# Window and global attention on one core: biases, output copies and shift pieces move to other engines, the ring of exponentials grows from eight to twelve units

## What is computed

```python
# layer 0, per window of 49 tokens
qn, kn = q / |q|, k / |k|
attn = softmax(qn @ kn.T * exp(min(logit_scale, log 100)) + bias[rel_index]);  h = proj(attn @ v)
h = relu(group_norm(x + h));  z = relu(group_norm(h + w2 @ relu(w1 @ group_norm(h) + b1) + b2))
# layer 1, per image, n = 3136 tokens, d = 16
q, k, v = split(w_qkv @ z)
attn = softmax(einsum("bhdn,bhdm->bhnm", q, k) * d ** -0.5)
out = w_proj @ einsum("bhnm,bhdm->bhdn", attn, v) + z
```

## Time and profile before

| | us |
|---|---|
| median of 3 runs | 8928.1 (8922.54 to 8929.63) |
| profiled execution, its run | 8930.84 |
| profiled execution, its span | 8928.7 |
| busy: PE, PEld | 8444.4, 4093.4 |
| busy: DVE, ACT, POOL | 7493.6, 6326.0, 835.1 |
| mean granted clock of TensorE | 0.98 |

### The profile page before, as it was taken

The page is one execution under the profiler, slowest core; times in us unless marked ns, Lnnn a source line. Parts: engine busy times, 40 slices in busy tenths (PEclk is TensorE's granted clock), DMA queues, the critical chain, the costliest instruction groups (busy, mean ns, idle before and its releaser), DMA issues.

```text
span 8928.7 us, 373040 instructions
## 1 busy us (share of the span) xinstructions
PE 8444.4 (95%) x145926; PEld 4093.4 (46%) x145926; DVE 7493.6 (84%) x9622; ACT 6326.0 (71%) x13874; POOL 835.1 (9%) x676
## 2 busy tenths in 40 slices
PE   4799999999999999999999999999999999999997
PEld 2344444444444444444444444444444444444443
DVE  3788888888888888888888888888888888888885
ACT  1377677776767777677776777767777776777776
POOL 3110101001010010101101010010100101010000
PEclk8799999999999999999999999999999999999998
DMA  1201102020110201102011110201102011020110
GB/s 32 40 14 27 27 20 37 12 38 18 28 28 15 41 15 27 27 13 42 14 26 27 23 34 12 42 17 25 28 15 40 15 27 27 13 43 13 29 23 19
DMA packets 123209, 226.00 MB, mean 25 GB/s; under 512 B 57218, under 2 KB 89090, under 8 KB 121354
## 3 DMA queue, kind: packets, MB, share of 16 engines
q1 hardware_dynamic: 121490, 201.52, 12.4%
HBM read 67.50 MB, written 42.73 MB: 12 GB/s over the span
## 4 chain that ended last, share of the span: by engine, by line
PE 76%; DVE 12%; issue 5%; SPq 3%; DMA 3%; ACT 1%; DVEq 0%; POOL 0%; POOLq 0%; ACTq 0%
PE PS L1251 22%; PE PS L1110 21%; PE PS L1263 20%; DVE small L891 7%; PE PS L1151 3%; PE PS L1171 3%; DVE small L930 2%; PE PS L1203 1%; DMA tok_unit<-in_query_ident 1%; PE PS L1141 1%; PE PS L1212 1%; SPq L619 1%; PE PS L1160 1%; PE PS L1182 1%; DVE win_scores L933 1%
## 5 line engine op out<-in xcount | busy, mean ns | idle before, releaser
L829 ACT ACTIVATE exps<-PS 128x392 f32<-128x392 f32 x12800 | 5502.0, 500 | 2087.5 <-PE PS L1251 1659.7
L891 DVE TENSOR_REDUCE small<-PS 128x1 f32<-128x784 f32 x6400 | 5878.1, 966 | 698.8 <-PE PS L1110 662.2
L1110 PE MATMUL PS<-k_stack,q_stack 96*32 96x392 bf16 x51200 | 3250.9, 334 | 225.5 <-DVE small L891 85.1
L1251 PE MATMUL PS<-q_stack,k_stack 99*32 99x392 bf16 x51200 | 3397.4, 333 | 26.9 <-ACT exps L829 12.6
L1263 PE MATMUL PS<-exps,v_all 128*32 128x392 f32 x25600 | 2687.4, 495 | 1.2 <-issue 1.0
L1251 PEld LDWEIGHTS PS<-q_stack,k_stack 99*32 99x32 bf16 x51200 | 1349.1, 95 | 1782.3 <-ACT exps L829 1033.2
L1110 PEld LDWEIGHTS PS<-k_stack,q_stack 96*32 96x32 bf16 x51200 | 1193.6, 96 | 1774.9 <-DVE small L891 967.6
L1263 PEld LDWEIGHTS PS<-exps,v_all 128*32 128x32 f32 x25600 | 749.6, 110 | 333.4 <-ACT exps L829 48.5
L729 POOL TENSOR_TENSOR win_scores<-win_scores,small 128x784 f32<-128x784 f32 x256 | 384.2, 1502 | 1860.0 <-DVE small L942 1860.0
L930 DVE TENSOR_REDUCE small<-PS 128x16 f32<-128x784 f32 x256 | 247.5, 967 | 182.6 <-PE PS L1151 181.2
L1151 PE MATMUL PS<-kmask,tok_unit 113*64 113x392 f32 (+1 forms) x2048 | 375.4, 502 | 16.5 <-DMA tok_unit<-in_query_ident 15.7
(11 more groups left out here) (113 smaller groups left out, 3044.9 us busy)
## 6 DMA issues: line engine op xcount, KB each, us to landing
q_stack<-tok_qk SPq DMA_DIRECT2D x320, 98.0 KB, 3.7
k_stack<-tok_qk SPq DMA_DIRECT2D x320, 98.0 KB, 4.2
kmask<-tok_unit SPq DMA_DIRECT2D x1024, 12.2 KB
att<-scratch_att SPq DMA_DIRECT2D x68, 196.0 KB
z_half<-scratch_z SPq DMA_DIRECT2D x34, 392.0 KB, 6.3
inv_sums<-scratch_rden SPq DMA_DIRECT2D x272, 49.0 KB, 2.1
scratch_att<-o_st SPq DMA_DIRECT2D x512, 26.0 KB
out<-inv_sums SPq DMA_DIRECT2D x68, 196.0 KB, 2.7
```

Source lines behind the costliest of these rows:

```text
L829: nc.scalar.activation(exps(u), PS[:, u % SCORE_BANKS, 0:GTOK], ACT.Exp, scale=D1 ** -0.5).then_inc(s_exps, 1)
L891: nc.vector.tensor_reduce(max_parts[:, n_:n_ + 1], slot(), op=ALU.max, axis=AX.XY)\
L1110: last = mm(PS[32 * r:32 * r + 32, it.bank + j, 0:GTOK], q_stack[0:STACK, stage // 2, q0:q0 + 32], k_stack[0:STACK, stage // 2, chunk * GT ...
L1251: last = mm(PS[32 * r:32 * r + 32, u % SCORE_BANKS, 0:GTOK], k_stack[0:STACK + SHIFT, h, k0:k0 + 32], q_stack[0:STACK + SHIFT, h, c * GTOK ...
```

## The change

`EXP_RING` becomes 12: the exponential of a quad's first unit waits for the weighing three quads back. Of `shift_pieces` only the negating reduction stays on VectorE, behind the stage's last maximum; the split becomes four GpSimd instructions (`pieces`), chained by a semaphore of GpSimd, the last subtraction writing its bf16 piece at once. The output copy of a stage and the bias of `qk` become ScalarE activations. The planner's `PARTS` are told so, and TensorE's order in `IMAGE_ORDER` and `LAST_ORDER` is another one, with the same numbers of each letter; `PROLOGUE_ORDER` stays.

```diff
-EXP_RING = 8
+EXP_RING = 12
...
-    "max": (("PE", 334), ("DVE", 884)), "shift": (("PE", 160), ("DVE", 220), ("SP", 2260)),
-    "copy": (("DVE", 560),), "store": (("SP", 1240),),
+    "max": (("PE", 334), ("DVE", 884)), "pieces": (("POOL", 1500),), "shift": (("PE", 160), ("DVE", 220), ("SP", 2260)),
+    "copy": (("ACT", 400),), "store": (("SP", 1240),),
...
-    "qk": (("PE", 660), ("DVE", 1040), ("POOL", 1450)), "sum": (("PE", 1320), ("DVE", 570)),
+    "qk": (("PE", 660), ("ACT", 720), ("POOL", 1450)), "sum": (("PE", 1320), ("DVE", 570)),
...
-SHIFT_PIECES = 1400
+NEGATE = 220
...
-            needs[at("exp", u)].append((at("weigh", u // 4 - 2), None))
+            needs[at("exp", u)].append((at("weigh", u // 4 - EXP_RING // 4), None))
...
-        needs[at("shift", stage)] = [(at("max", *STAGE_MAXIMA[stage][-1]), None)]
+        needs[at("pieces", stage)] = [(at("max", *STAGE_MAXIMA[stage][-1]), None)]
+        needs[at("shift", stage)] = [(at("pieces", stage), None)]
...
 IMAGE_ORDER = (
-    "MssMsMsssMWssMsMssWMssMssMWMsssMsMssWMMssWsssMsMssWMsMssWMsssMsMWMsssMsMWMsssMsqqqqsssMWMsMMsssWuMMWMMsssHMsssWs"
...
+    "MsssMMMsssMssMssMsssMssMWMMWMssMssMssWMssMsWMMWMMsssMWMssMssMsssMsMWMsssqqsssMWsMqqMsssWsWsussMMWsMMWsHsMsssssWs"
+    "spppMsWssMWMsssMssMsMsssMWMsssMWMskkssWsspsssMWsWsssMMsWsssttssskksssvsssMWMWssssMMsssWoMssWMsssMWMssttssMWMssMW"
+    "MsssMWMsssMsMsssMWssMkkssWsssMWWoMsssvMsssWssMssMssttssMWMssossMkksssWWWMMssssWMssstMssMsMssWsMktsWssMksssWsssWs"
+    "sHMsMsWMsssossjjWsttMssMssWMksskssvssMWssMsWssWoMsssMWMsssttsskkssWsssoWssMMsWMssstMssWMsssMWMsstMWsMsskksWsssWM"
...
+                elif it.kind == "pieces":
+                    shift_pieces(it.i, shift_count(it, b))
...
+            def shift_pieces(stage, count):
+
+                t0, t1 = STAGE_TILES[stage % 2]
+                nt = t1 - t0
+                high, middle, low = (neg_pieces[:, pc * nt:(pc + 1) * nt] for pc in range(3))
+                value, rest = neg_max[:, t0:t1], neg_rest[:, t0:t1]
+                wait_apart(pl, s_max_negated, count)
+                nc.gpsimd.tensor_copy(high, value).then_inc(s_shift_chain, 1)
+                pl.wait_ge(s_shift_chain, (count - 1) * 3 + 1)
+                nc.gpsimd.tensor_tensor(rest, value, high, ALU.subtract).then_inc(s_shift_chain, 1)
+                wait_apart(pl, s_shift_chain, (count - 1) * 3 + 2)
+                nc.gpsimd.tensor_copy(middle, rest).then_inc(s_shift_chain, 1)
+                pl.wait_ge(s_shift_chain, (count - 1) * 3 + 3)
+                nc.gpsimd.tensor_tensor(low, rest, middle, ALU.subtract).then_inc(s_max_pieces, 1)
...
+                elif it.kind == "qk":
+                    if it.i == 0 and not isinstance(t, int):
+                        for h in range(H1):
+                            act.wait_ge(s_stacks[h], t * 192)
+                    act.wait_ge(s_qk_product, t * 4 + it.i + 1)
+                    nc.scalar.activation(both_sides(tok_qk, it.i), PS[:, it.bank:it.bank + 2, 0:GTOK], ACT.Identity,
+                                         bias=bqk0).then_inc(s_qk_biased, 1)
+                elif it.kind == "copy":
+                    copy_half(it.i, b)
...
-                    act.wait_ge(s_pv_done, b * QUADS + u // 4 - 1)
+                    act.wait_ge(s_pv_done, b * QUADS + (u - EXP_RING) // 4 + 1)
...
+            def copy_half(stage, b):
+
+                act.wait_ge(s_pv_done, (b * STAGES + stage + 1) * TILES)
+                if stage == 0:
+                    act.wait_ge(s_out_stored, b * 512 + STORED)
+                else:
+                    act.wait_ge(s_out_stored, (b * STAGES + stage - 1) * 64 + STORED)
+                nc.scalar.activation(o_st[:, stage % 2, :], PS[:, PV_BANK, 0:GTOK], ACT.Copy).then_inc(s_out_copied, 1)
...
-                        shift_pieces(stage, b + 1 if stage == 0 else b)
+                        t0, t1 = STAGE_TILES[stage % 2]
+                        nc.vector.tensor_reduce(neg_max[:, t0:t1], max_parts[:, t0 * PAIRS:t1 * PAIRS]
+                                                .rearrange("p (t q) -> p t q", q=PAIRS), op=ALU.max, axis=AX.X,
+                                                negate=True).then_inc(s_max_negated, 1)
...
-                    nc.vector.tensor_scalar(both_sides(tok_qk, it.i), slot(), bqk0, None, ALU.add)\
-                      .then_inc(s_qk_biased, 1)
...
-                nc.vector.tensor_copy(o_st[:, stage % 2, :], PS[:, PV_BANK, 0:GTOK]).then_inc(s_out_copied, 1)
```

More of the change, by code:

```diff
@@ new lines @@
+    "ssMWMssMWssMMWMsssMsgsssMMWssMsMsssMWMWMsssMsgssMMsWMsssMsssMMWssMMWssssMMWsssWssMMsssWMsssMWgssMMssWMssMsssMssM"
+    "MWMsssMWMsssgsMMssWsssMMWMMWsMMsssaMsssWMsssWsssWsssHMsMsssMssMsMWMWMssasMWMsssMWMssMssMsssMWMssMsWMsMsssMWMWMMs"
+    "ssaasMMWMssMssMsssMWssMbbsssMWMsssMsMWMsssMWMssMssMsssaassMWMssMWMsssaasssMWMssMsWMssMsWsssWsssMssWsssMWssMMssWs"
+    "ssMbbsMssWssHsMFsssMWMsWsMMssWsssMMWsssMWMssMssWMMsssWMsgsssMMssWsssMMWsMsssMWsMssMWMsssMsgsssMMssWsssMMssWsMMWM"
+    "sssMWMsssMWMsssMsMsssMWMssMssMWMsssMWssMsMssWMsszzsssWMWsssFssWWssMssMsMsssMWMsssMWssHsMMsssWMssMWMsssMWsMssMWsM"
@@ L285, in follow @@
             offered[e].remove(n)
-            duration += SHIFT_PIECES * (kind == "max" and step[1:] == STAGE_MAXIMA[step.i][-1])
+            duration += NEGATE * (kind == "max" and step[1:] == STAGE_MAXIMA[step.i][-1])
         free[e] = begin + duration
@@ L426, in attention_mlp_kernel @@
         s_stacks = [sem(f"stacks_loaded{h}") for h in range(H1)]
-        s_max_filled, s_max_taken, s_max_pieces, s_shift_rows, s_shift_copied, s_shift_loaded = (sem(n) for n in (
-            "max_filled", "max_taken", "max_pieces", "shift_rows", "shift_copied", "shift_loaded"))
+        s_max_filled, s_max_taken, s_max_negated, s_max_pieces, s_shift_rows, s_shift_copied, s_shift_loaded = (sem(n) for n in (
+            "max_filled", "max_taken", "max_negated", "max_pieces", "shift_rows", "shift_copied", "shift_loaded"))
         s_scores, s_exps, s_pv_done, s_out_copied, s_out_stored = (sem(n) for n in (
@@ L436, in attention_mlp_kernel @@
             "final_proj", "final", "out_written"))
-        s_dve_chain, s_shift_chain = sem("dve_chain"), sem("dve_shift_chain")
+        s_dve_chain, s_shift_chain = sem("dve_chain"), sem("pool_shift_chain")
         CHAIN = 53
@@ L902, in step @@
                                           PS[0:3 * (t1 - t0), it.bank, 0:64].bitcast(bf16)).then_inc(s_shift_copied, 1)
[L903 to L906, removed]
-                    dve.wait_ge(s_qk_product, t * 4 + it.i + 1)
-                    nc.vector.tensor_scalar(both_sides(tok_qk, it.i), slot(), bqk0, None, ALU.add)\
-                      .then_inc(s_qk_biased, 1)
                 elif it.kind == "sum":
@@ L916, in step @@
                     nc.vector.reciprocal(tok_h[:, 0:GTOK], tok_h[:, 0:GTOK]).then_inc(s_norms_inverted, 1)
-                elif it.kind == "copy":
-                    copy_half(it.i, b)
                 elif it.kind == "spread":
```

56 lines of the change are left out of this document (17 added, 39 removed).

## The result

| | before | after |
|---|---|---|
| median, us | 8928.9 (10 runs, 8920.9 to 8937.1) | 8950.9 (10 runs, 8942.4 to 8961.5) |
| profiled execution, span | 8928.7 | 8950.9 |
| busy DVE, ACT, POOL | 7493.6, 6326.0, 835.1 | 7217.6, 6375.5, 939.1 |

A forecast was written before the change was run, and what follows sets the result against it. TensorE was taken as the bound, waiting 44 us a pass, mostly through VectorE. 8930.8 less 165 (VectorE), less 30 (ring), plus 15 (ScalarE) gave 8751, forecast as 8745 us; range 8560 to 8925.

The forecast's parts named there:

- What bounds the kernel: Loop pass: TensorE has at most 497 of 540.6 us of work and waits about 44; VectorE is next by load.
- I take 11 us a pass, near the middle: 165 us: VectorE: of 18.4 us an image taken off, between 3 us a pass and all of it shortens the pass.
- I take nothing for this by itself: TensorE's new order: same kinds and numbers of steps, same price, so 0 us.
- Hardly any instruction that stays on VectorE is of the kinds named: VectorE beside GpSimd: GpSimd's new pieces could hardly delay VectorE through shared ports; no term changes.
- what would be lost without the rule: VectorE: without the shared-port rule, 1.6 us a pass might fall on another instruction, losing 24 us of gain.
- The ring: Exponentials' ring of twelve: most ScalarE waits for weighings go, 330 to under 100 us; gain 2 us an image, 30 in all.
- ScalarE's times and the pieces: ScalarE: biases 922 ns, copies 500 ns, costing 1 us an image, 15 in all; GpSimd: four pieces 1.2 us, hidden, 0.
- (a): Only what stands on the chain counts, the rest becomes VectorE idle time: gain 45 us, 8883; chance 0.18.
- (c): No change: waits are a score's round trip through three banks; 8928 us, give or take 15; chance 0.09.
- (d): Slower: ScalarE's added biases and copies hold up exponentials and scores; costs 123 us against 45 gained, 9006; chance 0.09.

The follow-up runs named there:

- the lock out: Changed kernel with the order strings of the kernel before and GpSimd's multiplication of 784 columns cut into seven of 112: 8926.3 us, ratio 0.9996.
- the fitted ones: Pass orders searched with the planner, ring of twelve: bias, copies and pieces left on VectorE, 8696.9 us; moved as in the change, 8669.9 us.

## Why the prediction was wrong

**What bounds the kernel: right in the numbers, wrong in what they were taken for.** TensorE waits about 44 us a pass. (The 1567.7 us are 17 groups on 16 lines; the sum stands.) I read the 86% of VectorE beside it as a cause. The last image, which I had quoted myself, already said that 93% need not hold TensorE up. Cutting VectorE's busy time in half won 9.8 of the 44 us.

**The first step that failed** is "I take 11 us a pass, near the middle: 165 us", for what is taken off VectorE. The middle between the chain's 3 us and the whole 18.4 had no row behind it. All the moves together, ScalarE's additions included, cost 2.2 us a pass under the old order (0.8 with the lock out), and gained 5.6 under the new one and 2.0 between the fitted ones. No single number can stand in this place of the sum, since the worth of the relief belongs to the order. That something stands on the chain is no lower bound either: the lock (1.82 us) and a bias stood there, and with both gone under the old order the pass was longer.

**The second** is "I take nothing for this by itself", of the order. Its size shows in two ways. From before to after over the runs that lie between, the ring gives -9 us, then the new order +118, then the moves -87: 22 in all. The other way round it is -9 for the ring, +28 for the moves and +4 for the order. With the lock cut out of the second way it is -9, +6.5 and +24.6. The moves and the order can't be priced apart, and I had priced one as if it stood alone, and the other at nothing. The strings stood in the diff, and so did the planner that judges them: by its costs the new pass ends 3.5 us later than the old one, on the chip 1.6.

**"Hardly any instruction that stays on VectorE is of the kinds named"** was false. The group norm's products of columns have two inputs in SBUF. In the run of the moves under the old order one of them was held for 1.55 us, at another place of the pass than the pieces had been. The sentence on what would be lost without the rule, 24 us, describes what happened under the old order, but by the rule and not against it. In the changed kernel no VectorE instruction is lengthened, so the 25 us of lock that the kernel before had are gone from VectorE. To TensorE they had been worth little: where the same lock goes under the old order, it is 0.4 to 0.7 us a pass earlier.

**The ring.** The waits for weighings went from 330 to 91 us, as said ("under 100"). That 2 us a pass of it reach TensorE was wrong in both directions: 0.7 us a pass under the old order (539.9 against 540.6, within the interval of no change), 7 between fitted ones. A longer ring gave room, and the gain came with an order that uses it.

**ScalarE's times and the pieces: right.** The activations added cost 912 and 498 ns, as taken. What they cost TensorE is not shown by itself; under the old order all the moves with the lock out cost 0.8 us a pass, where I had taken 1 for ScalarE alone. The four pieces on GpSimd take 0.2 us each, and the last of them is over about 1.0 us after the first starts (346.9 to 347.7 plus 0.21); 1.2 was taken, and no wait of TensorE for it is in the trace:

```profile
L761 POOL CAST neg_pieces<-small x128: 191/197/206, 346.9 to 8846.8; 128x13 bf16<-128x13 f32 x64, 128x12 bf16<-128x12 f32 x64
...
L767 POOL TENSOR_TENSOR neg_pieces<-small,neg_pieces x128: 206/210/218, 347.7 to 8847.6; 128x13 bf16<-128x13 f32 x64, 128x12 bf16<-128x12 f32 x64
```

**The rivals.** (a), the relief becomes idle time of VectorE, named what happened under the old order and priced it with a gain of 45 us; (c), no change, gave 8913 to 8943, nearer to the result than any other. (d), ScalarE late, ended on the right side for the wrong reason. The waits of the weight loads of scores for exponentials did rise, from 1033.2 to 1082.5 us or 3 us a pass. But 2 of these come with the new order alone (1065.2), and under the old order the moves lowered them. None held that the order of the change could be the worse one. The range ended at 8925 because every case but (d) was given a gain or nothing.

**Where the new order loses.** Its stages differ from the old ones by -6.0 to +5.3 us each (71.1 and 67.5 us for the third and fifth, 77.1 and 62.2 before), most of it steps of layer 0 that stand elsewhere. One place stands out. `sum` (line 1134) needs GpSimd's squares of all four `qk` steps, 1.5 us each. Between the last q and the u of the strings lie 3.8 us of TensorE's steps in the old order and 2.5 in the new one (MsssWsWs), by the prediction's prices with 0.17 a score. TensorE's wait for the squares (us, times, longest) and the durations of the line from 500 to 8000 us, before and then after:

```profile
PE PS L1134 <- POOL tok_h L712: 13.1, 13, 2.8
L1134 PE MATMUL PS<-tok_h,w_head_sum x224: 492/492/518, 941.7 to 7972.2; 128*32 128x392 f32 x112
```

```profile
PE PS L1134 <- POOL tok_h L713: 32.8, 16, 3.0
L1134 PE MATMUL PS<-tok_h,w_head_sum x224: 492/512/861, 941.0 to 7991.7; 128*32 128x392 f32 x112
```

That is 1.2 us a pass more of waiting, and it is the order's: 17.1 us with the old order and the moves, 28.6 with the new order and the engines as before. In 8 of 14 passes the granted clock is at 0.50 for 3.4 us behind this wait, which it never is before. Over the 14 passes it is at 0.50 for 160 us instead of 116, 3.2 us a pass, of which by an estimate half is lost. Both together are more than the 1.6 us, so other places must win something back. No kernel with only this place changed was run, so that it makes the difference stays open.

## What to carry to other kernels

Before work is moved off an engine that looks nearly full, measure what its time is worth: cut its largest instruction short and look at the pass, and look for the single instructions that a busier engine waits for, since their worth can be far above the average. Where a fixed order feeds several engines through rings of two and three places, the order is the resource: refit it after every change of a buffer or an engine, judge old and new by the same measure, and don't judge the change by an order written for something else. A gain that changes its sign with the order may be a collision or may be load that stands elsewhere. Two sums that agree don't tell which; two traces with the same order, laid against each other step by step, do.

## What was not expected of the hardware

TensorE stands still at the turn of the loop, and around it runs at half its clock. In the kernel before (timeline of TensorE around the turn of one pass; then windows with length, busy times and, third from the end, the granted clock):

```profile
3065.38 0.52 PE L1110 MATMUL PS<-k_stack,q_stack 96*32 96x392 bf16 x8 [3.44 <-issue]
...
3068.61 0.52 PE L1110 MATMUL PS<-k_stack,q_stack 96*32 96x392 bf16 x3 [2.07 <-issue]
```

```profile
3055.00:3061.00 6.00, 6.00 (x120) 2.80 (x112) 5.01 (x7) 5.17 (x12) 0.00 (x0) 1.00 0.01 1
3061.00:3065.00 4.00, 0.93 (x12) 0.16 (x8) 1.41 (x2) 0.00 (x1) 0.52 (x1) 1.00 0.09 21
...
3069.00:3072.00 3.00, 3.00 (x40) 1.74 (x36) 2.16 (x3) 1.77 (x4) 0.00 (x0) 0.50 0.08 14
3072.00:3075.00 3.00, 3.00 (x49) 1.59 (x44) 1.59 (x2) 1.46 (x4) 0.00 (x0) 0.71 0.39 102
3075.00:3080.00 5.00, 4.99 (x96) 2.28 (x92) 5.00 (x7) 3.63 (x10) 0.00 (x0) 1.00 0.69 179
```

It stands for 3.44 and 2.07 us with nothing to wait for that the profile shows. Between the two stands the granted clock is still near full (0.98 from 3065 to 3067 us). It falls in the second one, and is 0.50, 1.2 instead of 2.4 GHz, until between 3072 and 3075. In the other passes the first stand is 3.4 to 4.0 us and the second 0.8 to 2.1, and the clock is at 0.50 for 6.8 or 10.2 us. So some 8 of the 44 us in a pass belong to the turn: about 5 of standing and, by an estimate, 3 to 4 lost to half speed. They are in the changed kernel as well (3.0 to 3.4 and 0.8 to 2.1 us of standing), which is one more reason why so little of the 44 was to be had.
